# Chunked delta-rule layer: joins of the inverse in 64x64 blocks, the solve in two halves, reordered queues

## The reference

```python
alpha = jax.nn.sigmoid(at + asp * spike)       # decay per head and channel
beta = jax.nn.sigmoid(bt[..., None] + jnp.sum(spike * bsp, -1, keepdims=True))
# state s (dk x dv per head) decays by alpha, then
# s += beta * k (v - k^T s)   and the output is q^T s
```

## Time and profile before

| | us |
|---|---|
| median of three runs (1457.33 to 1476.28) | 1461.54 |
| profiled execution | 1458.59 |
| its span, first to last instruction | 1456.9 |
| PE busy / DVE busy / ACT busy | 1115.5 / 1032.8 / 625.4 |
| mean granted PE clock | 0.868 |

### The profile page before, as it was taken

One profiled execution on the slowest core, in us unless ns is written; L12 is line 12 of the kernel. 1 busy time (PEld: TensorE's weight loads), 2 busy tenths in 40 slices (PEclk: granted clock), 3 DMA queues, 4 the chain that ended last, 5 costly groups with the idle time before them and its releaser, 6 DMA issues. The chain is left out here.

```text
span 1456.9 us, 23383 instructions
## 1 busy us (share of the span) xinstructions
PE 1115.5 (77%) x7956; PEld 821.2 (56%) x7956; DVE 1032.8 (71%) x3377; ACT 625.4 (43%) x860; POOL 57.4 (4%) x74
## 2 busy tenths in 40 slices
PE   2087777228888988889888898887876888889885
PEld 1043232117777877778777787777732635446381
DVE  4779999978788787887878878788241736454451
ACT  2247677323333433334333343333333656474522
POOL 2000000010000000000000000000100102011100
PEclk9579887558999999999999999999878998998956
DMA  2002233310100100101010010110110000000000
GB/s 84 0 1 87 105 127 145 116 51 16 36 25 33 36 14 36 35 22 36 14 36 36 22 36 14 36 36 7 30 39 0 1 0 8 0 8 1 8 1 7
DMA packets 27211, 49.09 MB, mean 34 GB/s; under 512 B 4246, under 2 KB 8919, under 8 KB 27162
## 3 DMA queue, kind: packets, MB, share of 16 engines
q1 hardware_dynamic: 25642, 47.02, 9.3%
q10 hardware_dynamic: 1520, 1.48, 0.4%
HBM read 26.47 MB, written 22.02 MB: 33 GB/s over the span
## 5 line engine op out<-in xcount | busy, mean ns | idle before, releaser
L920 PE MATMUL ps<-delta_tm,drive 128*128 128x128 f32 x768 | 106.7, 295 | 3.9 <-DVE delta_zb L1046 3.8
L920 PEld LDWEIGHTS ps<-delta_tm,drive 128*128 128x128 f32 x768 | 98.2, 205 | 9.4 <-DVE delta_zb L1046 5.9
L931 PE MATMUL ps<-delta_tt,delta_xf 128*128 128x64 f32 x768 | 101.4, 275 | 0.0
L929 PE MATMUL ps<-delta_xf,delta_tt 128*128 128x64 f32 x768 | 99.8, 273 | 0.0
L929 PEld LDWEIGHTS ps<-delta_xf,delta_tt 128*128 128x128 f32 x768 | 94.7, 194 | 0.0
L779 ACT ACTIVATE delta_xf<-ps 128x256 f32<-128x256 f32 (+1 forms) x128 | 49.1, 383 | 106.0 <-PE ps L920 86.0
L1203 DVE TENSOR_TENSOR delta_tm<-delta_tm,ps 128x256 f32<-128x256 f32 x96 | 40.3, 419 | 76.6 <-PE ps L931 75.6
L931 PEld LDWEIGHTS ps<-delta_tt,delta_xf 128*128 128x128 f32 x768 | 93.5, 192 | 0.0
L892 PEld LDWEIGHTS ps<-delta_kq_up,delta_arena 64*128 64x128 f32 x1024 | 74.1, 225 | 22.3 <-DVE delta_diag L1161 15.1
L892 PE MATMUL ps<-delta_kq_up,delta_arena 64*128 64x128 f32 x1024 | 80.3, 317 | 1.4
L551 DVE SCALAR_TENSOR_TENSOR kept<-mem 128x32 f32<-128x32 f32 x384 | 73.2, 191 | 1.6 <-PEq L79 1.0
(11 more groups left out here) (368 smaller groups left out, 2628.9 us busy)
## 6 DMA issues: line engine op xcount, KB each, us to landing
kq_store<-prep_unit SPq DMA_DIRECT2D x8, 1024.0 KB, 4.2
zb_store<-prep_zb_cols SPq DMA_DIRECT2D x8, 1024.0 KB, 5.7
delta_zb<-zb_store SPq DMA_DIRECT2D x16, 512.0 KB, 3.4
delta_kq<-kq_store SPq DMA_DIRECT2D x16, 512.0 KB, 3.2
v_store<-prep_v_rows SPq DMA_DIRECT2D x4, 1024.0 KB, 6.6
delta_v<-v_store SPq DMA_DIRECT2D x16, 256.0 KB, 2.6
out<-post_rows SPq DMA_DIRECT2D x4, 256.0 KB, 2.3
setup_wmod<-in_L_wmod ACTq DMA_DIRECT2D x2, 384.0 KB, 3.9
```

The source lines that it names most:

```text
L920: ins = eng.matmul(m.ps[:, 4 + n, P * (h % 4):P * (h % 4) + P], bt[s][:, h, :], m.tm[:, h, :], start=True, stop=True)
L929: eng.matmul(m.ps[:, 6 + n, HD * (h % 4):HD * (h % 4) + HD], m.tt[:, h, :], cols(m.xf[:, h, :], 0), start=True, stop=True)
L931: ins = eng.matmul(m.ps[:, 6 + n, 256 + HD * (h % 4):256 + HD * (h % 4) + HD], m.xf[:, h, :], cols(m.tt[:, h, :], 1), start=True, stop=True)
```

## The change

- `JOINS` is 8, 16, 32. In `join`, head 0 of each half keeps its whole tile; the other three heads multiply two 64 x 64 diagonal blocks (`tiles`). At level 32 only XT is made, no TX. `last_join` is gone.
- The solve is in halves: `solve_half(0)` gives u for steps 0 to 63, `carried` multiplies it with `bt[64]` and DVE subtracts it from the lower half of `rest`, `solve_half(1)` gives the others. In each half of the heads, head 0 again uses all 128 rows. `out_half` splits the output product by columns. The `seen` products move between X32 and XT32.
- The query parts of levels 32 and 64 are copied by ACT (`far_queries`), no longer by DVE. `tt` is made in two pieces.
- Orders change: on DVE `front_spikes` is made two chunks ahead, after join 8; `front_decay` comes before join 8a, `rest` before join 32a. On ACT the gates come before the copy of X8a, with their second half between X8a and X8b. On SP nothing is moved, POOL's program is unchanged.
- In `post_phase`, `contract` waits for each of its four inputs by itself; ACT copies the first attention weights earlier; PE's `y_sums` and `values` are interleaved anew; in the last round PE gets 16 products whose results nobody reads (`unread`).

```diff
-JOINS = [8, 16, 32, 64]
+JOINS = [8, 16, 32]
...
+            def far_queries(i):
+                eng.wait_ge(vector_back, vec.at("up16b", i))
+                for n, x in enumerate(HALVES):
+                    hs = slice(n, H, 2)
+                    ps = m.ps[:, BANK_OF[64] + n, :].rearrange("p (h a c) -> p h a c", h=4, a=2)
+                    eng.activation(m.a_qk[0:HD, hs, HD:P], ps[0:HD, :, 1, :], ACT.Copy).then_inc(scalar_back, act.one(f"qk64{x}"))
+                for n, x in enumerate(HALVES):
...
+                    eng.activation(m.a_qk[0:32, hs, 32:64], ps[0:32, :, 1, 0:32], ACT.Copy)
+                    eng.activation(m.a_qk[64:96, hs, 96:128], ps[64:96, :, 1, 32:64], ACT.Copy).then_inc(scalar_back, act.one(f"qk32{x}"))
...
+            def tiles(n):
+                whole, parts = slice(0, P), (slice(0, HD), slice(HD, P))
+                return [(4 * n, whole)] + [(h, ks) for h in range(4 * n + 1, 4 * n + 4) for ks in parts]
...
-                    for h in range(4 * n, 4 * n + 4):
-                        ins = eng.matmul(m.ps[:, 4 + n, P * (h % 4):P * (h % 4) + P], bt[s][:, h, :], m.tm[:, h, :], start=True, stop=True)
+                    for h, ks in tiles(n):
+                        c = P * (h % 4)
+                        ins = eng.matmul(m.ps[ks, 4 + n, c + ks.start:c + ks.stop], bt[s][ks, h, ks], m.tm[ks, h, ks], start=True, stop=True)
...
+            def solve_half(i, which):
+                ks = slice(HD * which, HD * which + HD)
+                eng.wait_ge(vector_back, vec.at("rest", i))
+                for n, x in enumerate(HALVES):
+                    eng.wait_ge(vector_back, vec.at(f"sub{x}" if which else f"XT{x}32", i))
+                    for h in range(4 * n, 4 * n + 4):
+                        rows = ks if h % 4 else slice(0, P)
+                        ins = eng.matmul(m.ps[ks, 4 * which + n, HD * (h % 4):HD * (h % 4) + HD], m.tt[rows, h, ks], m.rest[rows, HD * h:HD * h + HD], start=True, stop=True)
+                    ins.then_inc(tensor_back, pe.one(f"u{which}{x}"))
+            def carried(i):
+                eng.wait_ge(tensor_back, pe.at("read", i))
+                for n, x in enumerate(HALVES):
+                    eng.wait_ge(scalar_back, act.at(f"u0{x}", i))
+                    for h in range(4 * n, 4 * n + 4):
+                        ins = eng.matmul(m.ps[:, n, HD * (h % 4):HD * (h % 4) + HD], bt[64][0:HD, h, :], m.u_rows[0:HD, HD * h:HD * h + HD], start=True, stop=True)
+                    ins.then_inc(tensor_back, pe.one(f"w{x}"))
...
+            def state(i):
+                end_keys(i)
+                solve_half(i, 0)
+                seen_by_q(i)
+                carried(i)
+                out_half(i, 0)
+                eng.wait_ge(scalar_back, act.at("kend", i))
+                solve_half(i, 1)
+                eng.wait_ge(scalar_back, act.at("u1b", i))
+                out_half(i, 1)
+                update(i)
...
+                front_decay(i + 1)
                 join(i, 8, "a")
+                front_mid(i + 1)
                 join(i, 8, "b")
-                front_decay(i + 1)
+                front_splits(i + 1, UPPER[:1])
+                if ahead:
+                    front_spikes(i + 2)
                 join(i, 16, "a")
-                front_mid(i + 1)
-                front_splits(i + 1, UPPER[:1])
+                front_splits(i + 1, UPPER[1:3])
                 join(i, 16, "b")
-                front_splits(i + 1, UPPER[1:])
+                front_splits(i + 1, UPPER[3:])
                 front_toend(i + 1)
+                rest(i)
                 join(i, 32, "a")
                 front_beta(i + 1)
                 join(i, 32, "b")
                 front_base(i + 1)
-                front_upper(i + 1, UPPER[:1])
-                rest(i)
-                front_upper(i + 1, UPPER[1:3])
+                carried(i)
+                front_upper(i + 1, UPPER[:2])
                 keep(i)
-                front_upper(i + 1, UPPER[3:])
+                front_upper(i + 1, UPPER[2:])
                 update(i)
...
+            def unread(n):
+                for _ in range(n):
+                    eng.matmul(m.ps[:, 7, :], m.ones[:, :], cols(m.hT, 0), start=True, stop=True)
-            def contract(bank, w, src, done, value):
+            def contract(bank, w, src, done, value, made):
                 for c in range(4):
+                    eng.wait_ge(*made(c))
                     ins_ = eng.matmul(m.ps[:, bank, :], w[:, c, :], src[:, c, :], start=(c == 0), stop=(c == 3))
```

More of the change, by code:

```diff
@@ L609, in delta_phase @@
             + "".join(f" up{s}{x}" for s in UPPER[2:] for x in HALVES) + " tra trb"
[L610 to L614, removed]
+            + "".join(f" X{s}a X{s}b" + (" seen" if s == 32 else "") + f" XTa{s} XTb{s}" for s in JOINS)
+            + " kend u0a u0b read wa wb u1a u1b out update",
+            "scalar_back": "spread bt32a bt32b bt64a bt64b qk64a qk64b qk32a qk32b tra trb" + "".join(f" X{s}a X{s}b" for s in JOINS) + " u0a u0b kend u1a u1b out",
+            "vector_back": "base0 base1 near0 base2 near1 base3 near2 near3 spread up8a up8b mul1 row1 up16a mul2 row2 up16b"
+            + "".join(f" mul{r} row{r}" for r in range(3, BASE)) + " tta ttb kq_all k_end"
             + "".join(f" TXa{s} XTa{s} TXb{s} XTb{s}" for s in JOINS[:-1])
-            + " rest keep update",
+            + " rest XTa32 XTb32 suba subb keep update",
             "tensor_front": "beta count",
             "scalar_front": "zb_e zb_ln beta_e lift_p lift_n lift_up lift_all last",
-            "vector_front": "spikes z b1 zfloor b0 log_a G mid"
+            "vector_front": "z b1 zfloor b0 log_a G mid"
             + "".join(f" lo{s} hi{s}" for s in UPPER) + " toend b3 beta_k km_base kq_base"
@@ L961, in solve @@
                 eng.wait_ge(vector_back, vec.at("rest", i))
-                eng.wait_ge(scalar_back, act.at("XT64b", i))
-                for h in range(H):
-                    ins = eng.matmul(m.ps[:, 5, HD * h:HD * h + HD], m.tt[:, h, :], m.rest[:, HD * h:HD * h + HD], start=True, stop=True)
-                ins.then_inc(tensor_back, pe.one("solved"))
+                for n, x in enumerate(HALVES):
[4 more added lines that the diff above has]
+                    ins.then_inc(tensor_back, pe.one(f"u{which}{x}"))
@@ L1232, in _ @@
             front_decay(0)
+            front_spikes(1)
             front_mid(0)
@@ L1243, in _, with chunk @@
             eng.wait_ge(small_ready, 4)
-            with eng.Fori(0, NT - 1) as i:
+            def chunk(i, ahead):
                 base(i)
@@ L1275, in _ @@
             rest(NT - 1)
+            for x in HALVES:
+                join(NT - 1, 32, x)
+            carried(NT - 1)
             keep(NT - 1)
@@ L1941, in _ @@
                     gate_in(j)
+                if not mix:
+                    eng.wait_ge(mix_scalar, mact.at("v2b", i))
+                    unread(1)
                 if win:
@@ L1988, in _ @@
                     mix_mean("n1", j)
+                else:
+                    unread(1)
                 if win:
@@ L1992, in _ @@
                     mix_var("n1", j)
+                else:
+                    unread(2)
                 if win:
                     win_var("n3", i)
+                if not mix:
+                    unread(3)
                 if mix:
```

238 lines of the change are left out of this document (114 added, 124 removed).

## The result

The changed kernel takes 1598.65 us (median of 4 runs, 1591.96 to 1607.1) against 1461.99 us: ratio 1.092, 95% interval 1.083 to 1.101. The forecast was 1383, range 1328 to 1438. The profiled execution has a span of 1598.4 us.

What follows compares the result with a forecast made beforehand. No engine was full: PE led in the delta phase's joins, DVE earlier in the chunk. Delta chunks -54, contractions and first weights -11, last round -12 made -77 us: forecast 1383, range 1328 to 1438.

Steps and rivals of the forecast that it cites:

- rival 2: Joins: clock falls in most chunks, one or two half-clock spells, chunk 43.5 to 45.1, total 1412 to 1438; chance 0.21.
- The schedule: Delta chunk, timed step by step from DVE's first base copy: period 41.7 us for 45.1, -54 us over 16 chunks.
- rival 3: X8 to update: PE stays at 0.50, chunk 60 at the extreme; with passing spells 47 to 48, 1485 to 1500; chance 0.06.
- A quarter: Joins: PE price of one quarter-tile product, taken as 0.053 us, bounds 0.027 and 0.107.
- A change of shape: Joins: PE cost of switching between whole and quarter tiles, taken as 0.17 us each, twice a set, bounds 0 and 0.22.
- rival 1: Joins: changes of shape nearly free, levels 8 and 16 take 3.2 us of PE, DVE sets the pace, 1345; chance 0.25.
- the forecast's join arithmetic: Joins 8 and 16: a set costs 0.87 us, so a level takes 5.2 us of PE where 5.4 stood.
- 1.00 but for short spells: Sign to look for: granted clock between X8 and update; under 0.8 in the joins would make the forecast wrong.
- -11: After the delta phase: contractions starting with finished pieces and earlier copy of first weights, bounds -18 and -5 us.
- -12: Last round: 16 unread matmuls in PE's waits keep the clock up, saving 12 us; bounds -25 and +14.
- the 1.7 of the forecast: After the delta phase: `gated_out` no longer waits 1.41 us, c0 and c1 fit there; -1.7 a round, -6.8 in four.
- The earlier copy of the first weights: After the delta phase: ScalarE copies them before the gate's Ln and two y logs; -1.05 in three rounds, -3.2 us.

Runs made afterwards that it cites:

- e1_whole: The changed kernel with the joins' products whole again (all four heads 128x128), everything else of the change kept: 1425.37 us, ratio 0.973.
- f2_twice: The changed kernel with each quarter product of the joins issued twice: 1585.94 us, one run.
- h4_quarters_8: g2_fill with quarter tiles for three of four heads at join 8 only, XT in reverse order: 1393.42 us, ratio 0.953.
- e2_mirror: The changed kernel with the XT products of joins 8 and 16 in reverse order, quarters first: 1592.16 us, ratio 1.086.
- g1_rows: e1_whole with the two half solves reading all 128 rows for every head: 1401.24 us, ratio 0.960.
- g2_fill: g1_rows with two unread products of 512 columns, in PE's waits before the transposes and before the first X8: 1394.38 us, ratio 0.956.
- h1_fill_spread: g2_fill with two more unread products of 512 columns in PE's wait before the spread: 1389.99 us, ratio 0.951.
- h3_gates_back: g2_fill with ScalarE's gates back behind both X8 copies and DVE's decay back behind join 8: 1406.16 us, ratio 0.965.
- e3_post: The kernel before up to the end of the delta phase, with the change's edits from there on: 1444.76 us, ratio 0.986.
- e4_before_quarters: The kernel before with only the quarter tiles in its joins 8, 16 and 32 (three of four heads): 1602.73 us, one run.
- f1_two_whole: The changed kernel with two of four heads whole in the joins and two in quarters: 1603.19 us, one run.

## Why the prediction was wrong

**The step that failed** is the argument against rival 2: "525.4 to 541.7 holds 1.00 with L929's and L931's half-filled products". Those are whole 128x128 weight tiles with fewer columns, and they were taken as evidence for quarter tiles. The schedule was then priced at full clock from X8 to `update`. Measured: 0.50 for 30.8 us in the chunk shown, and 173 us of the whole time came back when the joins had whole tiles again (e1_whole). A nearer row had been in the text, the last round at 0.50 with PE busy 28.8 of 30.1 us. It is no quarter work either, but a good part of it has weights of 32 or 64 rows and only 32 or 64 moving columns, as PE's timeline there shows:

```profile
1388.41 1.98 PE L1880 MATMUL ps<-post_kc,hh 32*128 32x64 f32 x32 [1.21 <-ACT post_pt L1657]
1390.32 3.63 PE L1914 MATMUL ps<-post_v,post_pt 64*128 64x32 f32 x32
```

It was given to rivals 2 and 3 with chances of 0.21 and 0.06. The fact came out as rival 3's mechanism, its size between that rival's two prices: chunk 55.1, for 47 to 48 and 60. That rival's 60 doubled all PE work of the stretch; measured, a set went from 0.83 to 1.40 and a level from 5.4 to 8.7.

**Prices.** A set of one whole tile and six quarters: 0.87 forecast, 0.83 measured at full clock. The two unknown terms in it were each a little off and cancelled in part. A quarter was 0.053 and is 0.06 (f2_twice). A change of shape was 0.17 and is 0.12: at full clock mirroring takes one change out of a set and brings 0.83 to 0.71 (h4_quarters_8); at half clock it is 0.16 (e2_mirror). The sum is then 0.213 + 6 x 0.06 + 2 x 0.12 = 0.81. The Trainium skill's page TensorEngine Tiling (Array Packing), section Tiling Modes, names a drain at a change of mode; the trace agrees, with these 0.12 us. So rival 1 (nearly free, 0.55 a set) is refuted, and the forecast's join arithmetic, no gain at levels 8 and 16, was right.

**The clock rule.** The page TensorE: Matmul & The Clock Gate of the Trainium skill, section Why this matters for your kernels, asks for a busy TensorE without long gaps. Here PE is busy 30.18 of 30.8 us and gets 0.50: the trace does not agree. Busy time as the profile counts it does not tell the clock.

**Orders and halves.** With the quarters out of joins and solve, the chunk is 42.4 (g1_rows) and 41.9 (g2_fill). The forecast had 41.7, but for a kernel with quarters, so the equal period is partly luck. What it can confirm are the steps that the kernels share, and DVE's waits in a chunk of g1_rows at full clock bear them out (`update` to `update`, 711.18 to 752.73, is 41.55 us):

```profile
736.04 0.42 DVE L1219 TENSOR_TENSOR delta_tm<-delta_tm,ps 128x256 f32<-128x256 f32 x1 [1.49 <-PE ps L950]
...
740.92 0.75 DVE L1232 TENSOR_TENSOR drive<-delta_v,ps 128x256 f32<-128x256 f32 x2 [0.73 <-PE ps L958]
...
747.18 0.42 DVE L1240 TENSOR_TENSOR drive<-drive,ps 64x256 f32<-64x256 f32 x1 [1.30 <-PE ps L985]
748.07 0.42 DVE L1240 TENSOR_TENSOR drive<-drive,ps 64x256 f32<-64x256 f32 x1 [0.47 <-PE ps L985]
```

Before join 16a, `rest` and the subtractions DVE waits 1.49, 0.73 and 1.77 us, for 1.3, 0.5 and 1.6 in the schedule. "1.00 but for short spells" came true only where joins and solve have whole tiles (g1_rows 0.93, g2_fill 0.96, h1_fill_spread 0.98). That the new order of gates and decay is worth its place was implied, and h3_gates_back shows it: 12 us.

**After the delta phase** -11 and -12 were forecast, -3.4 and -12.5 measured in the kernel before; behind the changed delta phase the two together brought -18.9 for -23. `gated_out` did what was said: in e3_post it follows the hidden products at once, while the kernel before waited 1.41 us.

```profile
1254.53 1.02 PE L1804 MATMUL ps<-post_xc_a,post_wff 128*128 128x512 f32 x2
1255.39 3.60 PE L1752 MATMUL ps<-drive,post_wff 128*128 128x512 f32 x8
```

From there to the round's end e3_post needs 1290.15 - 1254.53 = 35.6 us, the kernel before 1294.03 - 1256.74 = 37.3: the 1.7 of the forecast. But from the round's start to the first hidden product it needs 1247.53 - 1207.19 = 40.3 for 38.5. The earlier copy of the first weights, priced at -1.05, comes with a new PE order, and together they cost 1.8. The clock goes with it: e3_post is granted 0.83 in these 40.3 us for 0.87 in the 38.5, and stands at 0.50 from 1227 to 1236, behind a wait of 1.85 us for ScalarE. Which of the two edits does it is open: they were not tried apart.

**What stays open.** Why quarters bring the clock down. It is neither the new order (e1_whole, e4_before_quarters) nor the changes of shape alone (e2_mirror: same clock with fewer; f2_twice: higher clock with as many). More products on the same tiles raise the clock (f2_twice), one level of quarters among whole tiles leaves it (h4_quarters_8), two of four heads in quarters at all levels lose it (f1_two_whole). A stream of quarters alone was not run. Nor was the size of the weights separated from the number of columns that move: a quarter moves 64 or 32 columns, a whole tile 128 or 64. The runs for f1_two_whole, f2_twice and e4_before_quarters are single ones; that the clock falls with quarters and comes back without them rests on the changed kernel against e1_whole, four runs each.

## What to carry to other kernels

Leaving out zero blocks pays only if PE is still the bound afterwards and keeps its clock: price the new stream at both clocks, and take the evidence for the clock from rows with the same tile shape. A chain of waits for copies between products (here 5.4 us at join 8 of h4_quarters_8) caps what faster products can give. Where the granted clock falls in a PE-bound stage, whole tiles over known zeros or an unread product in an existing wait can be the cheaper choice: here 1598.7 became 1425 and 1401 us with whole tiles and 1390 with fillers on top, by adding work.

## What the runs showed of the hardware

A busy PE can be granted half the clock: 0.50 for 30.8 us with PE busy 30.18, and 0.64 over 876 us with PE busy 791.87. Adding quarter products (f2_twice) raised the clock from 0.64 to 0.81 at about the same time, 1585.9 for 1598.7. A change between whole and quarter tiles cost 0.12 us at the full clock and 0.16 at half, and a set of mixed tiles slowed by 1.7 at half clock, not by 2. In the last round 16 unread products of 512 columns raised it from 0.60 to 0.86 and took 12.5 us off.
